# Products that nobody reads, put into TensorE's waits at the borders of a decoder layer's stages

## The reference

```
x = x + attn(layernorm(x), w_qkv, w_out)                    # first
x = x + xattn(layernorm(x), ctx, pos, Wq, Wkv, Wout, bout)  # cross
h = rms(layernorm(x), w_ln1)                                # rotary
x3 = layernorm(x) + attention(rope(h@wq+bq), rope(h@wk+bk), h@wv+bv) @ wo
h = rms(x3, w_ln2)
x = x + x3 + routed_experts(h, top 2 of 8) + sigmoid(h@w_sh_eg) * shared_expert(h)
```

## Time and profile before

| what | value |
|---|---|
| median of 3 runs | 2267.69 us (2266.1 to 2270.49) |
| profiled execution, its own time | 2264.66 us |
| profiled execution, span | 2262.8 us |
| mean granted clock of TensorE | 0.945 |
| PE busy | 2050.2 us (91%), 10679 matmuls |
| DVE busy | 1236.0 us (55%) |
| ACT busy | 880.9 us (39%) |
| POOL busy | 707.4 us (31%) |

### The profile page before, as it was taken

The page is one execution under the profiler, slowest core; times in us unless marked ns, Lnnn a source line. Parts: engine busy times, 40 slices in busy tenths (PEclk is TensorE's granted clock), DMA queues, the critical chain, the costliest instruction groups (busy, mean ns, idle before and its releaser), DMA issues. The chain is left out here.

```text
span 2262.8 us, 31473 instructions
## 1 busy us (share of the span) xinstructions
PE 2050.2 (91%) x10679; PEld 1371.7 (61%) x10679; DVE 1236.0 (55%) x2679; ACT 880.9 (39%) x1662; POOL 707.4 (31%) x610
## 2 busy tenths in 40 slices
PE   6998999877689999996987999969999988899998
PEld 5876666565433434334776666657888777565554
DVE  5546666477689798875876666534323242222221
ACT  3335544343368676773333544424222211011111
POOL 0004655256513232322554655501000000133332
PEclk9997999989789999997997999989999998999999
DMA  5457765355644546444457766461112053333332
GB/s 191 169 199 157 161 153 125 115 184 211 250 116 117 138 115 151 102 126 118 175 198 227 153 155 153 105 238 58 47 47 75 1 213 119 106 62 58 63 66 36
DMA packets 150514, 297.15 MB, mean 131 GB/s; under 512 B 24338, under 2 KB 42900, under 8 KB 149332
## 3 DMA queue, kind: packets, MB, share of 16 engines
q1 hardware_dynamic: 112772, 241.77, 36.6%
q10 hardware_dynamic: 28848, 34.74, 6.0%
q0 software_dynamic: 8736, 18.62, 4.5%
HBM read 181.55 MB, written 102.50 MB: 126 GB/s over the span
## 5 line engine op out<-in xcount | busy, mean ns | idle before, releaser
L1168 ACT ACTIVATE cross_c_prob<-bank 128x512 f32<-128x512 f32 x512 | 270.9, 598 | 117.9 <-PE bank L1007 116.8
L1207 DVE TENSOR_REDUCE cross_c_row_max<-bank 128x2 f32<-128x1024 f32 x256 | 300.0, 1212 | 29.3 <-PE bank L976 22.7
L1589 PE MATMUL bank<-moe_hT,moe_w 128*128 128x512 f32 x1056 | 259.8, 403 | 2.2 <-DVE moe_hT L1831 2.2
L1007 PE MATMUL bank<-stack 56*128 56x512 f32 (+4 forms) x768 | 234.4, 429 | 20.8 <-DMA stack<-rotary_c_max_rows 7.9
L976 PE MATMUL bank<-stack 48*128 48x512 f32 (+4 forms) x768 | 212.5, 457 | 37.2 <-PEq L70 19.7
L1589 PEld LDWEIGHTS bank<-moe_hT,moe_w 128*128 128x128 f32 x1056 | 205.4, 196 | 46.8 <-DVE moe_hT L1831 2.6
L1007 PEld LDWEIGHTS bank<-stack 56*128 56x128 f32 (+1 forms) x768 | 119.6, 193 | 151.3 <-ACT cross_c_prob L1168 70.0
L1677 PE MATMUL bank<-moe_w_e,moe_hT_e 128*128 x624 | 194.5, 465 | 2.3 <-DMA moe_w_e<-in_experts_packed 1.9
L976 PEld LDWEIGHTS bank<-stack 48*128 48x128 f32 (+1 forms) x768 | 104.6, 202 | 121.3 <-DVE cross_c_row_max L1207 53.3
L1203 DVE CUSTOM_DVE_ANT_0 first_c_masked<-bank,later 128x128 f32<-128x128 f32 (+3 forms) x256 | 115.8, 486 | 78.0 <-PE bank L976 77.0
L1677 PEld LDWEIGHTS bank<-moe_w_e,moe_hT_e 128*128 128x128 f32 x624 | 116.2, 191 | 64.3 <-issue 6.3
(11 more groups left out here) (344 smaller groups left out, 4037.8 us busy)
## 6 DMA issues: line engine op xcount, KB each, us to landing
moe_w_e<-in_experts_packed SPq DMA_DIRECT2D x8, 2176.0 KB, 9.0
qk_parts<-first_p_parts SPq DMA_DIRECT2D x32, 512.0 KB, 2.7
stack<-qk_parts SPq DMA_DIRECT2D x64, 256.0 KB, 6.8
qk_parts<-cross_p_parts SPq DMA_DIRECT2D x32, 512.0 KB, 2.7
stack<-qk_parts SPq DMA_DIRECT2D x256, 64.0 KB, 2.5
qk_parts<-rotary_p_parts SPq DMA_DIRECT2D x32, 512.0 KB, 2.7
moe_raw<-in_shared_packed SPq DMA_DIRECT2D x11, 768.0 KB, 11.0
stack<-qk_parts SPq DMA_DIRECT2D x16, 512.0 KB, 5.2
```

The costliest lines, as they stand in the source:

```text
L1007: last = nc.tensor.matmul(bank[:, 0 : S - q0], k_stack[slot][r : r + ALL_ROWS, at, m * P : (m + 1) * P], q_stack[slot][r : r + ALL_ROWS, a ...
L1168: nc.scalar.activation(probability(g, step // HEADS_AT_ONCE, step % HEADS_AT_ONCE), psum[bank_at["score", n]][:, 0 : S - q0], ACT.Exp).the ...
L1207: nc.vector.tensor_reduce(row_max[:, g % 2, m, j - 1 : j + 1], c.banks[:, first : first + WIDE, :], AX_X, ALU.max).then_inc(s.max_done, 1)
L1589: last = nc.tensor.matmul(psum[bank][:], weights(pa, f, k), hT[p % 2][:, pb, k, :], start=m == 0, stop=m == len(steps) - 1)
```

## The change

A function `keep_warm` issues products of the identity with itself, 512 columns wide unless told otherwise, into a bank that nothing reads before it is written anew. It waits for nothing and signals nothing. It is called:

- at the start of each projection phase: 3 products behind the first `turn_in`, and in the first phase 5 more ahead of it;
- at the end of each projection phase, behind the last tile: 3, 9 and 6 products (first, cross, rotary);
- at the start of each core: one product of 256 columns behind every second score tile of the 16 of group 0 and of the 10 or 12 of group 1, then 3, 0 and 4 products of 512 columns ahead of the first `scoresT`;
- at the end of each core, behind `project_last`: 9, 13 and 10 products;
- in the MoE phase: 2 products behind the first two `turn_two`.

```
+def keep_warm(nc, c, bank, products, columns=4 * P):
+    for _ in range(products):
+        nc.tensor.matmul(bank[:, 0:columns], c.ident[:], c.ident[:].unsqueeze(1).to_broadcast([P, columns // P, P]), start=True, stop=True)
...
# projection_phase
+        WARM_AT_END = {"first": 3, "cross": 9, "rotary": 6}[a.kind]
...
+                    if turning:
+                        keep_warm(nc, c, psum[7], 5)
                     turn_in(0)
+                    keep_warm(nc, c, psum[7], 3)
                     for n, (bi, what, m) in enumerate(ring):
...
+                    keep_warm(nc, c, psum[0], WARM_AT_END)
...
# core_phase
+        WARM_AT_START, WARM_AT_END = {"first": (3, 9), "cross": (0, 13), "rotary": (4, 10)}[a.kind]
...
                     for i in range(N16):
                         scores(0, i)
+                        if i % 2:
+                            keep_warm(nc, c, psum[bank_o], 1, 2 * P)
                     for i in range(a.lead):
                         scores(1, i)
+                        if i % 2:
+                            keep_warm(nc, c, psum[bank_o], 1, 2 * P)
                         if i == 2:
                             max_transpose(0)
+                    keep_warm(nc, c, psum[bank_o], WARM_AT_START)
                     for g in range(GROUPS):
...
                     project_last()
+                    keep_warm(nc, c, psum[7], WARM_AT_END)
...
# moe_phase
                 turn_two(0, 0)
                 turn_two(0, 1)
+                keep_warm(nc, c, psum[SG], 2)
```

## The result

| what | before | after |
|---|---|---|
| median of the runs on one chip | 2266.89 us (2262.51 to 2270.49) | 2299.3 us (2292.45 to 2305.13) |
| ratio, 95% interval | | 1.0147 [1.0125, 1.0169] |
| profiled execution, span | 2262.8 us | 2296.0 us |

A forecast was written before the change was run, and what follows sets the result against it. TensorE, busy 91% of the span, was taken as mostly bounding the kernel. Gains of 13.0 us against losses of 23.2 made it 10.2 later: 2274.9, or 2277.9 by the median, stated as 2277 us; 8-in-10 range 2262 to 2290.

The forecast's parts named there:

- The meeting waits for TensorE's unread products, at 0.86 us each.: Ends of the three cores: all engines wait for TensorE's last product; DVE starts 5.4, 9.8 and 6.7 us later, together 21.9.
- The clock gets nothing for it.: Behind the cores' ends: TensorE is idle again before the next transposes (447.7 to 455.0 in cross), so no clock gain.
- In cross a pair of score tiles and one narrow product take about 0.9 us at full clock: Cross core's first scores: hidden below DVE's 1.18 us at full clock; at half clock 1.7, and 0.5 us a pair shows.
- the clock isn't held: Rival, chance 0.12: narrow products too thin or cores start at half clock; gains near 0, 2298 us by the median.
- Causal first groups, 3.6 and 2.6 us.: First scoresT groups of the first and rotary cores: gains of 3.6 us (0 to 6.6) and 2.6 (0 to 5.5).
- Rotary projection, 2.2 us.: Start of the rotary projection: first v product sooner, limited by its weights being ready; gain 2.2 us, bounds 0 and 2.3.
- Cross projection, 2.4 us less 0.5 at its end.: Cross projection: first 12 products gain 2.4 us (0 to 2.6) from the clock; its end loses 0.5 (0 to 5.4).
- Launch: First projection: launch products gain 0.7 us (0 to 1.7) from the clock; the products at its end lose 0.8.
- the upper bounds of its gains: Largest gains allowed for launch, projections and cores, summed there to 22.2 us against the 13.0 expected.

The follow-up runs named there:

- both_off: The change without its products at the cores' ends and without the narrow products among the cross core's first scores; 2261.11 us, 0.9967 of the kernel before.

## Why the prediction was wrong

Right, by its steps:
- *The meeting waits for TensorE's unread products, at 0.86 us each.* 22.5 us in the trace for 21.9, 25 and 26 us in two timed experiments. Shown by taking them out, putting them in alone and making them short.
- *The clock gets nothing for it.* The wait ahead of the transposes and their half clock are still there behind all three cores.

Wrong:
- *"In cross a pair of score tiles and one narrow product take about 0.9 us at full clock (2 x 0.22 + 0.43), below DVE's 1.18, and are hidden."* This is the step that failed. At full clock it is right (1.06 us), but the clock is lost in TensorE's wait for the first maxima, isn't regained, and at 0.50 the pair with its product takes 1.88 us, and DVE waits. The trace has 9.6 us, the timed runs 9 us (put in alone), 15 and 16 (taken out, with and without the products at the cores' ends; differences of two ratios, each uncertain by 3 to 5 us). The rival "the clock isn't held" named the half clock and 2298 us; I gave it 0.12, though the only row on that stretch, 37.4 us at half clock, spoke for it, and the earlier trace rows had the wait for stores in which the clock then fell. Its price was too low as well: 1.7 us a pair by columns and clock, where 1.88 was measured, and 0.5 times 14 against some 0.66 (1.88 - 1.22) times 14, 9.2. That its 2298 is near the measured 2299 is partly luck: it had no gains, where 7.5 us were measured, and 7 us for the narrow products.
- *Causal first groups, 3.6 and 2.6 us.* Both were taken as the distance to the next group, 12.2 us. With the clock at 0.88 a first group still takes 14.4 us, no less than the other's 14.3 at 0.65, and 1.4 and 0.3 came in these profiles. The prediction named the copies of the output weights that ACT makes beside the exps, and counted them at nothing; TensorE's waits for ACT in that group fit them (2.6 us), but no run takes the copies away. The timed run of this part shows no gain.
- *Rotary projection, 2.2 us.* Its first v product does come 1.9 us sooner (25.3 us behind the clear, 27.2 before), but the whole projection is not shorter. Of the 1.9 only 0.3 is left 86 us behind the clear, and there, across the next transposes, the distance between two products grows from 3.6 to 5.3: TensorE waits 1.9 us for DVE's rows and not 1.3, and 12 transposes take 2.75 us and not 1.53. Given back inside the stage.
- *Cross projection, 2.4 us less 0.5 at its end.* 2.8 us from clear to clear in this pair of profiles, 4.4 by the means over all: the right way, and its size is uncertain by some us. So it belongs to what was right. *Launch*: 0.3 us longer for a predicted 0.1, nothing to tell apart.

The sum as measured: 26 and 9 us put in alone, or 25 and 15 taken out, for the core ends and the narrow products, less 7.5 of gain from all the rest (13.0 predicted): 27 to 33 of the 33 us. The difference is inside the intervals.

One sum of the prediction is off by a little: the upper bounds of its gains add up to 22.4 and not 22.2. Nothing hangs on it.

## What to carry to other kernels

A product that nobody reads is free only where nobody waits for TensorE itself: at a meeting of all engines its queue counts, so such products belong behind the meeting, in the wait for the next stage's rows. Before a stretch is counted as held at full clock, look at the waits inside it and at whether the trace ever shows this very sequence at full clock; where it doesn't, price the added work at half clock against the engine that it hides behind. The same instructions at full clock elsewhere in the stage say nothing of it. And the distance from a slow first round to the next one is not what the clock costs: look at what else that round does.

## What was not expected of the hardware

- Clock at 0.50 for 74.9 us with TensorE busy in all of it, where 512-column products over all 128 rows alternate with score tiles over 48; the same products in a row raise it to 0.90 over 8.3 us.
- Alternating one-pass products of 512 columns with different weights are 0.72 us apart at half clock, where a pair of score tiles in different halves of the rows took 0.73 together (608.24 to 608.97 in the profile after) and 12 projection products took 0.43 each.
- 16 transposes take 2.03 us at full clock and 3.67 at half. In both_off the transposes alone raise the clock: behind a wait of 9.50 us, 24 of them run from 443.23 to 447.95, and the clock is 0.50 until 447.3 and 1.00 from 447.6.
